# A transformer kernel on one core: the last attention sequence written out, the first MLP chunk shifted and centred in it, and the drain of the attention reordered

## The reference, cut to what matters

```
for i in range(6):
    x = attn_layer(shift_tokens(x), Wqkv[i], q_scale[i], k_scale[i], Wo[i]) + x
    x = ffn_layer(shift_tokens(x), ln_g[i], ln_b[i], W1[i], b1[i], W2[i], b2[i]) + x
```

## Time and profile before

| | |
|---|---|
| time, median of 3 runs | 4024.63 us (4024.32 to 4025.49) |
| the profiled execution's own time | 4030.75 us |
| its span, first to last instruction | 4028.8 us |
| mean granted TensorE clock | 0.982 |
| busy share of the span | PE 95%, VectorE 78%, ScalarE 74%, GpSimd 63% |
| one step of the attention pipeline in the loop | about 7.09 us |

### The profile page before, as it was taken

One profiled execution on the slowest core, in us unless ns is written; L12 is line 12 of the kernel. 1 busy time (PEld: TensorE's weight loads), 2 busy tenths in 40 slices (PEclk: granted clock), 3 DMA queues, 4 the chain that ended last, 5 costly groups with the idle time before them and its releaser, 6 DMA issues. The chain is left out here.

```text
span 4028.8 us, 155156 instructions
## 1 busy us (share of the span) xinstructions
PE 3808.7 (95%) x61323; PEld 2394.8 (59%) x61339; DVE 3127.4 (78%) x4956; ACT 2966.2 (74%) x6599; POOL 2520.9 (63%) x2418
## 2 busy tenths in 40 slices
PE   6997797999999999999999999999999999999998
PEld 3665684666645666546666456666466664566663
DVE  5886565899957999758999579998489995699984
ACT  5885214888876888768888668887688887688885
POOL 3553233788835888627888358887178884488870
PEclk8999997999999999999999999999999999999999
DMA  2000000000000000000000000000000000000000
GB/s 75 0 0 1 0 0 6 1 0 0 0 22 7 0 0 0 22 6 1 0 0 0 22 7 0 0 0 22 6 1 0 0 0 22 7 0 0 0 22 21
DMA packets 12345, 27.34 MB, mean 7 GB/s; under 512 B 2460, under 2 KB 6728, under 8 KB 11344
## 3 DMA queue, kind: packets, MB, share of 16 engines
q1 hardware_dynamic: 12240, 25.72, 1.8%
HBM read 23.62 MB, written 2.10 MB: 6 GB/s over the span
## 5 line engine op out<-in xcount | busy, mean ns | idle before, releaser
L950 POOL TENSOR_TENSOR w_t<-w_t 128x512 f32<-128x512 f32 x768 | 979.3, 1285 | 515.9 <-DVE w_t L1252 515.9
L1252 DVE TENSOR_TENSOR w_t<-banks,w_tab 128x512 f32<-128x512 f32 x1536 | 955.9, 684 | 235.7 <-ACT w_sq L1390 227.0
L966 POOL TENSOR_TENSOR w_t<-w_t,w_rn 128x512 f32<-128x512 f32 x768 | 784.4, 1042 | 251.6 <-ACT w_rn L1427 251.6
L1044 PE MATMUL banks<-w_qk,w_xs 128*128 128x512 f32 x1536 | 825.2, 620 | 9.7 <-issue 8.6
L1064 PE MATMUL banks<-w_vo,w_xs 128*32 128x256 f32 x12288 | 823.1, 385 | 4.9 <-ACT w_us L1381 4.8
L1052 PEld LDWEIGHTS banks<-ident,w_t 128*128 128x128 f32 x3072 | 380.2, 140 | 432.5 <-issue 413.8
L1381 ACT ACTIVATE w_us<-banks 128x512 f32<-128x512 f32 x768 | 458.2, 597 | 162.2 <-PE banks L1064 157.5
L1052 PE MATMUL banks<-ident,w_t 128*128 128x128 f32 x3072 | 461.7, 273 | 25.3 <-POOL w_t L966 16.7
L1064 PEld LDWEIGHTS banks<-w_vo,w_xs 128*32 128x32 f32 x12288 | 321.6, 109 | 243.1 <-issue 77.2
L1289 DVE TENSOR_REDUCE w_ss<-w_sq 128x16 f32<-128x1024 f32 x384 | 464.9, 1211 | 0.0
L971 POOL TENSOR_TENSOR w_pr<-w_pr,w_rl 128x512 f32<-128x512 f32 x384 | 402.4, 1048 | 87.2 <-ACT w_rl L1432 87.2
(11 more groups left out here) (178 smaller groups left out, 5973.0 us busy)
## 6 DMA issues: line engine op xcount, KB each, us to landing
w_qk<-w_qk_in SPq DMA_DIRECT2D x7, 1024.0 KB, 4.8
w_v<-w_v_in SPq DMA_DIRECT2D x7, 512.0 KB, 5.6
w_o<-w_o_in SPq DMA_DIRECT2D x7, 512.0 KB, 6.4
m_w<-m_w_in SPq DMA_DIRECT2D x6, 342.0 KB
xT<-x_in SPq DMA_DIRECT2D x4, 512.0 KB
out<-kept SPq DMA_DIRECT2D x8, 256.0 KB, 2.6
m_w<-m_w_in SPq DMA_DIRECT2D x6, 171.0 KB
r_tab<-r_tab_in SPq DMA_DIRECT2D x1, 512.0 KB
```

The lines of the kernel that those rows point to most:

```text
L950: nc.gpsimd.tensor_tensor(v1, v1, v2[:, :, ::-1, :], ALU.add).then_inc(S["added"], 1)
L966: nc.gpsimd.tensor_tensor(v1, v1, rn[j % 2][:, i * HALF:(i + 1) * HALF].unsqueeze(2) .broadcast_to([P, HALF, WD]), ALU.mult).then_inc(S["n ...
L1044: nc.tensor.matmul(banks[:, i, :], x[:], wqk[:, i * INNER + hh * C:i * INNER + (hh + 1) * C], start=True, stop=True).then_inc(S["qk"], 1)
L1252: nc.vector.tensor_tensor(dst[j % 2][:, i * C:(i + 1) * C].rearrange("p (h d) -> p h d", d=WD), src, tab[:, 2 * t + cs, i * WD:(i + 1) * W ...
```

## The change

- `pipeline` writes out the last sequence too (`final` is true in it). The loop is one sequence shorter.
- ScalarE shifts chunks 0 and 1 in steps 1 and 2 of that last sequence. PE centres chunk 0 in its step 3, between the scores and the second half of the values, and ScalarE squares it there.
- PE's drain: variance of chunk 0 is moved up to step 0, between the two groups of transposes; centre of chunk 1 is moved to behind the transposed probabilities of step 1; variance of chunk 1 and `up(0, 0, 2)` come behind the transposes of step 2.
- ScalarE's drain: the exponential comes first, then `invert(0)` without a table load, then the two copies; `square(1)` comes ahead of the Gelus; `invert(1)` comes later in step 2.
- PE's wait for all attention results is taken from the head of the MLP stage and put into each `down` with `k == 1`.

The rest of the diff only passes the new argument through every engine's `iteration`.

```diff
@@ -875,13 +875,15 @@
 
     def pipeline(eng, layer, iteration):
 
-        def one(j, seq, live):
-            iteration(j, seq, lambda lag: layer * N + seq * STEPS + (j - lag + 1), live)
+        def one(j, seq, live, last=False):
+            iteration(j, seq, lambda lag: layer * N + seq * STEPS + (j - lag + 1), live, last)
         for j in range(STEPS):
             one(j, 0, lambda lag: lag <= j)
-        with eng.Fori(1, B) as seq:
+        with eng.Fori(1, B - 1) as seq:
             for j in range(STEPS):
                 one(j, seq, lambda lag: True)
+        for j in range(STEPS):
+            one(j, B - 1, lambda lag: True, True)
         for j in range(LAG):
             one(j, B, lambda lag: lag > j)
 
@@ -940,7 +942,7 @@
                         pool.wait_ge(M["shifted"], passed(made + 1 + back))
                         pool.sem_inc(sem("gate"), 1)
 
-                def iteration(j, seq, n, live):
+                def iteration(j, seq, n, live, final):
                     j2 = (j - 2) % STEPS
 
                     def add(i, name):
@@ -1027,6 +1029,8 @@
 
                 def down(c, k):
                     pe.wait_ge(M["residual"], finished(layer, c - 1))
+                    if k == 1:
+                        pe.wait_ge(S["residual"], passed((layer + 1) * B * TILES))
                     for m in range(MG):
                         pe.wait_ge(M["made"], passed((done + c) * MG + m + 1))
                         pe.sem_inc(sem("gate"), 1)
@@ -1151,24 +1155,27 @@
                             pe.wait_ge(S["q_rotated"], passed((n(0) - 1) * 2))
                         pe.sem_inc(sem("gate"), 1)
                         project(0)
+                    if tail and j == 0:
+                        variance(0)
                     if live(1):
                         turn(1)
-                    if tail and j == 2:
-                        variance(1)
                     if live(4) and j % 2 == 1:
                         pe.wait_ge(S["y_taken"], passed(tiles(layer, j, seq, 4)))
                         pe.sem_inc(sem("gate"), 1)
                         nc.tensor.transpose(banks[:, 7, P:2 * P], ysb[:], ident[:]).then_inc(S["y_turned"], 1)
                     if live(3):
                         turn_probabilities()
-                    if tail and j < 2:
-                        centre(j, j, True)
+                    if tail and j == 1:
+                        centre(1, 1, True)
                     if tail and j == 2:
+                        variance(1)
                         up(0, 0, 2)
                     if live(0):
                         values(0)
                     if live(1):
                         scores()
+                    if final and j == STEPS - 1:
+                        centre(0, 0, True)
                     if live(0):
                         values(1)
                     if live(3):
@@ -1176,8 +1183,6 @@
                     if tail and j == 1:
                         pe.wait_ge(S["centred"], passed((layer + 1) * N * 2))
                         up(0, 0, 1, True)
-                    if tail and j == 0:
-                        variance(0)
 
                 pipeline(pe, layer, iteration)
 
@@ -1189,8 +1194,6 @@
                     up(c, k, 2)
                     down(c - 1, 1 - k)
 
-                pe.wait_ge(S["residual"], passed((layer + 1) * B * TILES))
-                pe.sem_inc(sem("gate"), 1)
                 pairs(pe, chunk)
                 up(NCH - 1, 1, 0)
                 up(NCH - 1, 1, 1)
@@ -1342,8 +1345,9 @@
                     act.wait_ge(M["centred"], passed(done + c + 1))
                     nc.scalar.activation(squares, banks[:, XC, :], ACT.Square).then_inc(M["squared"], 1)
 
-                def invert(c):
-                    nc.scalar.preload_act_table_set("natural_log_exp_and_others")
+                def invert(c, load=True):
+                    if load:
+                        nc.scalar.preload_act_table_set("natural_log_exp_and_others")
                     act.wait_ge(M["var"], passed(done + c + 1))
                     nc.scalar.activation(logs, banks[:, VAR, :], ACT.Ln, bias=eps_col[:]).then_inc(M["logged"], 1)
                     act.wait_ge(M["logged"], passed(done + c + 1))
@@ -1381,8 +1385,6 @@
                         nc.scalar.activation(us[j][:, 2 * a:2 * a + 2].rearrange("p w a n -> p (w a n)"),
                                              banks[:, 2, :], ACT.Copy).then_inc(S["u_taken"], 1)
 
-                    if tail and j < 2:
-                        shift_chunk(j)
                     if live(0):
                         act.wait_ge(S["qk"], passed(n(0) * 2 - 1))
                         if live(1):
@@ -1397,26 +1399,38 @@
                         act.wait_ge(S["qk"], passed(n(0) * 2))
                         nc.scalar.activation(sq[:, 0].rearrange("p h d -> p (h d)"), banks[:, 0, :], ACT.Square)\
                             .then_inc(S["q_squared"], 1)
-                    if live(1):
+                    def take_keys():
                         hk, lo = j1 % 2, WIN + (j1 // 2) * P
                         act.wait_ge(S["turned"], passed(n(1) * 2))
                         nc.scalar.activation(kT[:, hk * NPAIR:(hk + 1) * NPAIR, lo:lo + P],
                                              banks[:, 4, :].rearrange("p (g k) -> p g k", k=P), ACT.Copy)\
                             .then_inc(S["k_turned"], 1)
-                    if live(3):
+                    def take_probabilities():
                         act.wait_ge(S["p_turned"], passed(n(3)))
                         nc.scalar.activation(prT[:].rearrange("p g q -> p (g q)"), banks[:, 3, :], ACT.Copy)\
                             .then_inc(S["p_taken"], 1)
-                    if tail and j == 2:
-                        invert(1)
-                    if tail and j == 0:
-                        square(0)
-                    if live(0):
-                        values(0)
-                    if live(2):
+                    def exponential():
                         act.wait_ge(S["centred"], passed(n(2) * 2))
                         p = pr[j2 % 2][:].rearrange("p a h r -> p (a h r)")
                         nc.scalar.activation(p, p, ACT.Exp).then_inc(S["exped"], 1)
+
+                    if tail:
+                        if live(2):
+                            exponential()
+                        if j == 0:
+                            invert(0, False)
+                        if live(1):
+                            take_keys()
+                        if live(3):
+                            take_probabilities()
+                    else:
+                        if live(1):
+                            take_keys()
+                        if live(3):
+                            take_probabilities()
+                        values(0)
+                        if live(2):
+                            exponential()
                     if live(0):
                         act.wait_ge(S["sums"], passed(n(0)))
                         nc.scalar.activation(lg[:], ss[j % 2][:], ACT.Relu, bias=floor[:, 0:1]).then_inc(S["guarded"], 1)
@@ -1439,17 +1453,21 @@
                             shift(1, seq)
                         else:
                             shift(0, seq + 1)
+                    if final and j in (1, 2):
+                        shift_chunk(j - 1)
+                    if final and j == STEPS - 1:
+                        square(0)
                     if live(0):
                         values(1)
+                    if tail and j == 2:
+                        invert(1)
                     if live(3) and j % 2 == 0:
                         act.wait_ge(S["valued"], passed(n(3)))
                         nc.scalar.activation(ysb[:], banks[:, 7, 0:P], ACT.Copy).then_inc(S["y_taken"], 1)
-                    if tail and j == 0:
-                        invert(0)
                     if tail and j == 1:
+                        square(1)
                         act.wait_ge(S["mlp_weights"], layer * 48 + 48)
                         gelu(0, 0, 0, True)
-                        square(1)
                         gelu(0, 0, 1, True)
                     if tail and j == 3:
                         gelu(0, 0, 2, True)
```

## The result

The kernel after takes 4001.62 us (median of 5 runs, 4000.66 to 4003.61), the kernel before 4024.63; the ratio is 0.9944, with a 95% interval of 0.9929 to 0.9958. That is faster by 23 us, where 59.6 were forecast, and it lies above the range (3948 to 3993). The profiled execution took 4002.89 us, its span 4000.9.

A forecast was written before the change was run, and what follows sets the result against it. PE, busy 95% of the span, was taken to bound the kernel, losing time in each layer's drain. Drain savings of 54.2 us plus 4.7 from the second slow stretch, off the 4024.6 median, gave 3965, range 3948 to 3993.

The forecast's parts named there:

- The written-out sequence: PE's instruction loading for the last sequence, each layer: taken as costing nothing, bounds nothing and 8.9 us in all.
- Code loading makes it slower: Rival: in the last sequence, five code blocks a layer each stop PE 2.4 us, 72 us in all, 4038; chance 0.04.
- The clock still falls: Rival: PE's new waits still leave the drain partly at 1.2 GHz, no second-stretch gain, 3986.8 us; chance 0.2.
- The second slow stretch: From centring of chunk 2 to first MLP add, layers 2 to 5: 9.3 us lost to slow clock, 4.7 taken back.
- The schedule: Drain, times of layer 0: forecast start times of each group, centring chunk 2 at 1150.5 instead of 1159.82, 9.3 us less.
- The 1.1 us wait: Drain step 0, ahead of PE's scores: replaces the 3.89 us wait, as the keys' copy queues behind `invert(0)` on ScalarE.
- The shift copies: Steps 1 and 2 of the last sequence: pairs cost 0.2 and 1.27 us, making scaling 1.45 us late; bounds 0 and 2.54.
- The table load: Load dropped from `invert(0)` in the drain: saves 1.28 us by the profile row, rather than the Trainium skill's 2.66.
- PE's moved wait: Wait for attention results, now in the second `down`, 10 us into the MLP stage: costed at nothing.
- only the 3.89 us wait is won: Rival: in the drain, ScalarE holds keys back and the delay repeats each step, so 4001 us; chance 0.12.

The follow-up runs named there:

- e9: Kernel after, with 100 idle PE instructions added in the very first block, where PE waits for the inputs: 3968.95 us, ratio 0.9861.
- e4: Kernel before, with only the last sequence written out and nothing else changed: 4044.13 us, ratio 1.0049.
- e12: Kernel after with 100 idle PE instructions in the first block, and the table load kept in `invert(0)`: 3985.62 us, ratio 0.9902.
- e1: Kernel after, with the next layer's attention weights loaded only when the second MLP chunk is through: 3979.58 us, ratio 0.9884.
- e10: Kernel after, with 20 idle PE instructions in the first block, where PE waits for the inputs: 3994.48 us, ratio 0.9928.
- e5: Kernel after, with 100 idle PE instructions put once in the first attention block, where PE waits for GpSimd: 3982.59 us, ratio 0.9896.

## Why the prediction was wrong

**What failed** is one term of the sum: "The written-out sequence ... I take nothing, as the straight code of sequence 0 is the nearest case", with 8.9 us as its upper bound. It had the number of transfers nearly right (some 30 more forecast, 24 measured) and their cost wrong. Straight code costs PE little while its blocks come in ahead of need (e9). In drain step 0 the scores and applied probabilities, 128 and 56 records in 1.9 us, end a block sooner than the next one comes, and here its transfer stood behind the weights. Sequence 0 was a poor stand-in: it has no large transfer beside it from its second step on. The term measures 22.2 us in pauses, and the clock falls behind each of them. The rival "Code loading makes it slower" had the mechanism but asked for five pauses a layer from the longest wait seen; there was one, and its size came from a transfer that the text had not put beside it: it noted neither that the weights are released by the last values nor when they run.

**The clock.** With a pause of 3.4 to 3.9 us in each drain the clock fell behind each, as the rival "The clock still falls" had it, but for another reason. The second slow stretch of the earlier trace rows did go: the first window of the MLP stage, where layers 2 and 3 had 13.58, takes 10.63 us at full clock in all six layers. That gives back all of the 9.3 us, of which the forecast took half. In e9 there is no slow stretch in any drain, and it is 32.7 us faster than the kernel after: 22.2 us of pauses and 10.5 for the clock and all else. The stretch that runs slowly, from the first `up` to the second, takes 6.1 to 7.1 us in the kernel after and 4.3 in e9, which is 13.9 us in six layers.

**What is left** against the forecast of 3965 is 4 us. In e9, PE still has short breaks (0.4 to 1.1 us a layer) in the last sequence, inside the applied probabilities or the values and with "issue" as their reason. From the first to the last square, the six attention pipelines take 4.9 us longer in e9 than in the kernel after, which has no such breaks there. So the 4 us fit these breaks; no run took them out.

**The schedule held.** Scores forecast at 1137.65, in the trace 1137.65; `up(0,0,0)` at 1139.6, in e9 1139.16; centre of chunk 2 at 1150.5, in e9 1150.63. The 1.1 us wait ahead of the scores was 1.02. The gain of 9.3 us a layer is there once the code is: in e9 chunk 2 is centred 9.2 us earlier than before.

**The shift copies.** GpSimd's scaling was forecast 1.45 us late and is 1.60 late (1132.85 for the 1131.25 of the earlier trace rows). The split held roughly too. From one step's first square to the next, the steps with the two pairs take 7.51 and 8.13 us in the kernel after, 7.13 and 7.09 before, and 7.12 and 7.10 in e4, where the sequence is written out without the copies. So the pairs cost 0.4 and 1.0 us where 0.2 and 1.27 were forecast, and this was no part of the miss.

**The table load.** The row's 1.28 us was right against the 2.66 of the Trainium skill (e12). But this load brings in the set that is already there, while the skill's figure is for a switch. For switches the trace after shows it: the loads at 1149.72 and 1153.21 us, to Gelu and back to Ln, are each followed by their function 1.30 us after they start. **PE's moved wait** shows no cost: in e9, PE has no idle time from the centring of chunk 2 at 1150.63 us to beyond 1180 us, and the first two `down` lie in that stretch.

**The rival that came nearest in time**, 4001 for "only the 3.89 us wait is won", had the wrong mechanism: ScalarE held nothing back beyond 1.0 us.

## What to carry to other kernels

Code is a transfer too. When a loop pass is written out next to a bulk load, ask which block of the list is needed while the load runs, above all for PE groups of many short matmuls; a break in the middle of a group, with no wait in the code and "issue" as its reason, is the sign. Moving the load shortened the break here; shifting the code by 100 idle instructions, put where the engine waits anyway, took it out of the drain and made a kernel of 3968.95 us from one of 4001.62. The number has to be tried (20 did not do it), and shorter breaks came up elsewhere. And a pause counts twice where the clock falls behind it: 1.3 us more idle time a layer in e12 cost 2.8.

## What was not expected of the hardware

- PE starved of code with no other transfer under way (e1): 1.46 us inside a group, at a fixed place in the list. With the weights in the way the place moved by 10 matmuls for 20 instructions (e10). The Trainium skill (page "Runtime: NRT & Kernel Launch", Instruction fetch mechanics) has the transfer of the next block mostly hidden, because issue is slower than the refill. That does not hold for this stretch; how far ahead a block is asked for was not measured.
- An instruction transfer is held up by ordinary transfers: none among 549 packets, then one, and a pause of 3.92 us for 1.46. How it is queued among them was not shown.
- A semaphore increment of PE's took 0.13 to 0.22 us when 100 stood in a row: 13.1 us more in e5, and all of them gone in the 21.7 us before PE's first matmul in e9.
- One alignment of the list against another was worth 33 us of 4000, with the same work in the same order.
